# Attention outputs scaled by the softmax reciprocals once a group, instead of the probabilities head by head

## The reference

```
L0: self-attention "a0" (16 heads of 16, latent keys and values, scores times exp(-0.01 |i-j|))
    cross-attention on 64 context rows, butterfly feed-forward
L1: self-attention "a1" (16 heads of 64, rotary position, causal)
    attention "x1" (8 heads of 64, keys and values of x and of the 64 context rows)
    mixture of experts (8 experts, top 2)

attention:  p = softmax(scale * q k^T)      one row of probabilities per query
            out = (p v) W_o
```

## Time and profile before

| | us |
|---|---|
| median of 3 runs (4370.3 to 4377.9) | 4376.41 |
| the profiled execution's own time | 4397.46 |
| its span | 4395.7 |
| stage a0, about | 17 to 955 |
| cross-attention, folding, feed-forward, about | 955 to 1462 |
| stage a1, about | 1462 to 2590 |
| stage x1, about | 2590 to 3400 |
| experts and the rest | 3400 to 4396 |
| PE busy, mean granted clock | 3439.4 (78%), 0.898 |
| DVE, ACT, POOL busy | 2820.9, 2073.9, 1385.9 |

### The profile page before, as it was taken

The page is one execution under the profiler, slowest core; times in us unless marked ns, Lnnn a source line. Parts: engine busy times, 40 slices in busy tenths (PEclk is TensorE's granted clock), DMA queues, the critical chain, the costliest instruction groups (busy, mean ns, idle before and its releaser), DMA issues. The chain is left out here.

```text
span 4395.7 us, 81705 instructions
## 1 busy us (share of the span) xinstructions
PE 3439.4 (78%) x25420; PEld 2507.5 (57%) x25421; DVE 2820.9 (64%) x7262; ACT 2073.9 (47%) x4994; POOL 1385.9 (32%) x1108
## 2 busy tenths in 40 slices
PE   5878788758689588888888879999998409999970
PEld 3555555537678356666556556777767306666650
DVE  5888888868867488888888846666666311121116
ACT  4777777753242165555555536555555101111110
POOL 1333333324300376666665702122222350000004
PEclk9999999988799799999899989999999559999995
DMA  2000000010010211111111110000000720010013
GB/s 68 6 7 7 7 7 7 1 34 19 25 74 1 66 44 35 30 44 37 35 40 31 33 41 7 11 6 6 6 1 1 242 80 27 29 31 29 29 35 105
DMA packets 101919, 147.71 MB, mean 34 GB/s; under 512 B 19904, under 2 KB 71552, under 8 KB 100800
## 3 DMA queue, kind: packets, MB, share of 16 engines
q1 hardware_dynamic: 95424, 126.58, 9.5%
q0 software_dynamic: 6144, 16.79, 1.2%
HBM read 61.52 MB, written 31.46 MB: 21 GB/s over the span
## 5 line engine op out<-in xcount | busy, mean ns | idle before, releaser
L1012 DVE TENSOR_SCALAR a_t<-a_t,a_inv 128x512 f32<-128x512 f32 (+3 forms) x768 | 719.1, 979 | 9.0
L695 PE MATMUL a_T<-ident,a_t 128*128 128x128 f32 x3328 | 535.3, 300 | 163.8 <-DVE a_t L1012 89.8
L854 ACT ACTIVATE a_t<-a_t,a_neg 128x512 f32<-128x512 f32 (+3 forms) x1024 | 642.5, 634 | 7.7 <-DVE a_neg L1040 7.3
L845 ACT ACTIVATE a_pT<-a_T 128x512 f32<-128x512 f32 (+3 forms) x1024 | 484.7, 514 | 328.1 <-PE a_T L695 324.6
L695 PEld LDWEIGHTS a_T<-ident,a_t 128*128 128x128 f32 x3328 | 402.7, 151 | 379.8 <-issue 217.0
L884 POOL TENSOR_TENSOR a_t<-a_t,a_inv 128x512 f32<-128x512 f32 x256 | 284.4, 1133 | 653.5 <-DVE a_inv L1008 653.5
L1035 DVE CUSTOM_DVE_ANT_0 a_t<-a_A,a_decay 128x512 f32<-128x512 f32 x512 | 322.7, 685 | 91.0 <-PE a_A L655 89.3
L884 POOL TENSOR_TENSOR x_t<-x_t,x_inv 128x576 f32<-128x576 f32 x128 | 158.1, 1257 | 696.3 <-DVE x_inv L1008 696.3
L2096 DVE COPY experts_y<-experts_Y 128x256 f32<-128x256 f32 x72 | 30.6, 425 | 513.9 <-PE experts_Y L2034 513.9
L909 POOL TENSOR_TENSOR a_rsin<-a_rawswapped,a_sin 128x512 f32<-128x512 f32 x128 | 170.1, 1329 | 583.5 <-DMA a_rawswapped<-a_raw 558.7
L1035 DVE CUSTOM_DVE_ANT_0 a_t<-a_A,a_table 128x384 f32<-128x384 f32 (+3 forms) x512 | 224.1, 485 | 128.5 <-PE a_A L667 125.6
(11 more groups left out here) (273 smaller groups left out, 7243.1 us busy)
## 6 DMA issues: line engine op xcount, KB each, us to landing
a_rawswapped<-a_raw SPq DMA_DIRECT2D x512, 64.0 KB, 2.0
ex_w<-in_f_w_dram SPq DMA_DIRECT2D x16, 1024.0 KB, 13.6
moe_sent<-route_zeros SPq DMA_DIRECT2D x1, 9216.0 KB, 29.5
experts_xg<-moe_sent SPq DMA_DIRECT2D x72, 128.0 KB, 2.0
moe_results<-experts_y SPq DMA_DIRECT2D x72, 128.0 KB, 1.7
a_xin<-x_all SPq DMA_DIRECT2D x16, 512.0 KB, 4.1
x_xin<-x_all SPq DMA_DIRECT2D x16, 512.0 KB, 2.9
x_all<-in_x_dram SPq DMA_DIRECT2D x1, 4096.0 KB, 14.9
```

What stands on the lines that cost most here:

```text
L695: mm = pe.transpose(bank[:, kt, :], t_of(u, j, kt * P, (kt + 1) * P), sh.ident[:])
L845: nc.scalar.activation(to, of, ACT.Copy).then_inc(t_empty, 1)
L854: nc.scalar.activation(t_of(u_e % U, j, 0, n), t_of(u_e % U, j, 0, n), ACT.Exp, bias=neg[:, slot, j:j + 1], scale=SCALE, accum_out=total[: ...
L1012: nc.vector.tensor_scalar(t_of(u_n % U, j, 0, m), t_of(u_n % U, j, 0, m), inv[:, u_n % 4, j:j + 1], None, ALU.mult).then_inc(normed, 1)
```

## The change

1. Nobody multiplies the probabilities. PE transposes them as soon as exp is done (it waits for `exped` instead of `normed`).
2. DVE still takes the reciprocals; `inv` now keeps all units of a batch. After each unit SP writes the 128x4 reciprocals to a table in DRAM, transposed, so that a row holds one head's 512 queries (`spill`). Once per SPAN units (8 in a0, 4 in a1 and x1) SP reads the rows back, each repeated over the partitions that the head's outputs take in O, into `inv_rep` (`spread_rows`: 8 transfers in a0, 2 otherwise), and waits for them.
3. The copy of O to `oT` moves from ACT to DVE and becomes a product with `inv_rep`. It stands after DVE's items of the step and before the score maxima, and waits for PE's product and for the spread.
4. SP's program becomes one list of steps: input load, spread, spill, then in a1 the swaps. POOL's program for a0 and x1 is gone.
5. The folding loads its weights in two parts a side, of 3 and 4 stages, not 2, 2 and 3.

```diff
@@ attention
-    POOL_HEADS = () if a1 else (2, 3)
-    DVE_HEADS = 4 - len(POOL_HEADS)
+    SPAN = 8 if a0 else 4
+    COPIES = 8 if a0 else 2
...
-        inv = sb("inv", [P, 4, 4])
+        inv = sb("inv", [P, U, 4])
+        inv_rep = sb("invrep", [P, 1 if a0 else 2, S])
+        inv_rows = nc.dram_tensor(f"{kind}_inv_rows", (2, SPAN, S), F32).ap()
...
+            def spill(b, u):
+
+                g, qt = divmod(u % U, QT)
+                rows = inv_rows[g // 2 % 2, g % 2::2] if a0 else inv_rows[g % 2]
+                wait_apart(sp, (weights, 16 * len(loads)), (inverted, b * U + (u + 1)))
+                sp.dma_start(rows[:, qt * P:(qt + 1) * P].rearrange("j p -> p j"), inv[:, u % U, :], allow_slow_non_contiguous=True)\
+                  .then_inc(spilled[u % U // SPAN % 2], 16)
+
+            def spread_rows(b, k):
+
+                per = U // SPAN
+                p = k % per % 2
+                wait_apart(sp, (weights, 16 * len(loads)),
+                           (spilled[p], b * (per // 2 * SPAN * 16) + (k // 2 + 1) * SPAN * 16))
+                for c in range(COPIES):
+                    if a0:
+                        to, of = inv_rep[16 * c:16 * c + 16, 0, :], inv_rows[p, c:c + 1, :].to_broadcast([16, S])
+                    else:
+                        to = inv_rep[64 * c:64 * c + 64]
+                        of = inv_rows[p, c::2, :].unsqueeze(0).to_broadcast([64, 2, S])
+                    sp.dma_start(to, of).then_inc(spread, 16)
+                wait_apart(sp, (weights, 16 * len(loads)), (spread, b * (per * COPIES * 16) + (k + 1) * COPIES * 16))
+
+            def step(b, s, prev, own, nxt):
+                if s == 0 and nxt:
+                    sp.wait_ge(xt_done, b * DT + DT)
+                    sp.dma_start(xin[:], sh.x_all[:, bass.ds(b * QT + QT, QT), :]).then_inc(xin_in, 16)
...
+                u_n = s - LAG_N
+                if s < U and u_n % SPAN == 0 and (own if u_n > 0 else prev):
+                    spread_rows(b, u_n // SPAN - 1)
+                if s < U and (own if u_n >= 0 else prev):
+                    spill(b, u_n)
+                for _, work in tasks(s, prev, own, nxt):
+                    if a1 and work[0] == "item":
+                        swap_halves(b + (work in NEXT and s >= U - QT), 4 * work[1] + work[2])
@@ PE, transpose_head
-                by_dve, by_pool = min(j + 1, DVE_HEADS), min(j + 1, 4) - DVE_HEADS
-                waits = [(normed, ug * DVE_HEADS + by_dve)] + \
-                    ([(normed_pool, ug * len(POOL_HEADS) + by_pool)] if by_pool > 0 else []) + [(t_empty, job + 1)]
...
+                wait_apart(pe, (ready, N_READY), (exped, ug * 4 + min(j + 1, 4)), (t_empty, job + 1))
@@ ACT, step
-                        act.wait_ge(pv, b * U + (u_v + 1 + 2))
-                        for o in ([g // 2] if a0 else [0, 1]):
-                            nc.scalar.activation(oT[:, o if a0 else 2 * g + o, :], O[o][:],
-                                                 ACT.Copy).then_inc(o_empty, 1)
@@ POOL: the step that multiplies heads 2 and 3, and its loop, are removed
@@ DVE, step
-                        nc.vector.reciprocal(inv[:, u_n % 4, :], total[:, u_n % 4, :]).then_inc(inverted, 1)
-                        dve.wait_ge(inverted, b * U + (u_n + 1))
-                    if do_n and j < DVE_HEADS:
-                        m = NK if x1 else keys(u_n % U)
-                        nc.vector.tensor_scalar(t_of(u_n % U, j, 0, m), t_of(u_n % U, j, 0, m),
-                                                inv[:, u_n % 4, j:j + 1], None, ALU.mult).then_inc(normed, 1)
+                        nc.vector.reciprocal(inv[:, u_n % U, :], total[:, u_n % 4, :]).then_inc(inverted, 1)
...
+                if do_v and u_v % SPAN == SPAN - 1:
+                    g = u_v % U // QT
+                    wait_apart(dve, (ready, N_READY), (pv, b * U + (u_v + 1 + 2)),
+                               (spread, (b * (U // SPAN) + (u_v + 1) // SPAN) * COPIES * 16))
+                    for o in ([g // 2] if a0 else [0, 1]):
+                        nc.vector.tensor_tensor(oT[:, o if a0 else 2 * g + o, :], O[o][:], inv_rep[:, 0 if a0 else o, :],
+                                                ALU.mult).then_inc(o_empty, 1)
                 if own:
 
                     dve.wait_ge(t_full, (b * U + s + 1) * T_UNIT)
@@ fold_butterflies
-        GROUPS_OF = ((0, 2), (2, 4), (4, 7))
+        GROUPS_OF = ((0, 3), (3, 7))
```

More of the change, by code:

```diff
@@ L331, in attention @@
         idle = {"a0": ("ctx_in", "v_done", "rot_sum", "rot_done", "biased", "q_low", "low", "kp"),
-                "a1": ("folded", "ctx_in", "kl_done", "kp", "q_low", "biased", "normed_pool", "hi"),
+                "a1": ("folded", "ctx_in", "kl_done", "kp", "q_low", "biased", "hi"),
                 "x1": ("folded", "a_act", "rot_sum", "rot_done", "kl_done", "low", "kp")}[kind]
@@ L419, in attention @@
         exped = sem("exped")
-        normed = sem("normed")
-        normed_pool = sem("normed_pool")
+        spilled = [env.sem(f"spilled{i}") for i in range(2)]
+        spread = sem("spread")
         t_full = sem("t_full")
@@ L496, in swap_halves @@
                                  raw[32 * (k ^ 1):32 * (k ^ 1) + 32, n % 4, :]).then_inc(swapped[n % 2], 16)
[L498 to L515, removed]
-                      .then_inc(ctx_in, 16)
+            def spill(b, u):
[4 more added lines that the diff above has]
+                  .then_inc(spilled[u % U // SPAN % 2], 16)
@@ new lines, in step @@
+            def step(b, s, prev, own, nxt):
+                if s == 0 and nxt:
+                    sp.wait_ge(xt_done, b * DT + DT)
+                    sp.dma_start(xin[:], sh.x_all[:, bass.ds(b * QT + QT, QT), :]).then_inc(xin_in, 16)
+                if x1 and s == LAG_V and nxt:
+                    sp.wait_ge(v_done, b * N_V + N_V)
+                    sp.dma_start(ctxT[:], w["ctxT"][bass.ds(b + 1, 1)].rearrange("a (t p) n -> p (a t) n", p=P))\
+                      .then_inc(ctx_in, 16)
+                u_n = s - LAG_N
[6 more added lines that the diff above has]
+                        swap_halves(b + (work in NEXT and s >= U - QT), 4 * work[1] + work[2])
@@ L518, in _, with begin, body @@
+            def begin():
+                for work in START:
+                    if a1 and work[0] == "item":
+                        swap_halves(0, work[2])
+            def body(seg, turn, b, prev, own, nxt):
+                for s in range(U if own else LN_STEP):
+                    step(b, s, prev, own, nxt)
+            batches(sp, begin, body)
         @block.tensor
@@ L877, in _ @@
         def _(pool):
[L878 to L883, removed]
-                        nc.gpsimd.tensor_tensor(t_of(u_n % U, j, 0, NK), t_of(u_n % U, j, 0, NK),
-                                                inv[:, u_n % 4, j:j + 1].to_broadcast([P, NK]),
-                                                ALU.mult).then_inc(normed_pool, 1)
-            def begin():
-                pool.wait_ge(ready, N_READY)
-            def body(seg, turn, b, prev, own, nxt):
-                for s in range(U if own else LN_STEP):
-                    step(b, s, prev, own, nxt)
-            if not a1:
-                batches(pool, begin, body)
             if a1:
@@ L940, in _ @@
             dve.sem_inc(a_dve, A_BANKS)
+            dve.sem_inc(o_empty, 2)
             def low_parts(seg, turn, b, g, i):
@@ L1002, in step @@
                 do_n = s < U and (own if u_n >= 0 else prev)
+                u_v = s - LAG_V
+                do_v = s < U and (own if u_v >= 0 else prev)
                 slot, qt, n = s % 4, s % QT, keys(s)
@@ L1402, in fold_butterflies @@
         T = [env.ps(f"T{i}", [P, S]) for i in range(2)]
-        GROUPS_OF = ((0, 2), (2, 4), (4, 7))
-        staged = [[sem(f"staged_{side}{i}") for i in range(3)] for side in ("up", "down")]
+        GROUPS_OF = ((0, 3), (3, 7))
+        staged = [[sem(f"staged_{side}{i}") for i in range(2)] for side in ("up", "down")]
         loaded_up = sem("loaded_up")
```

4 lines of the change are left out of this document (removed).

## The result

Measured side by side on one chip, the changed kernel takes 4725.99 us (median of four, 4715.43 to 4754.48), the kernel before 4373.35 (4366.06 to 4377.9): a ratio of 1.082, 95% interval 1.077 to 1.087. The forecast was 4181 us, its range ended at 4310. The profiled execution took 4722.31 us, with a span of 4720.5.

What follows compares the result with a forecast made beforehand. It took x1 as bound by PE, a0 and a1 by engines holding one another up. Terms -100 - 86 - 16 + 5 + 2 = -195 us took 4376.4 to 4181 us; range 4060 to 4310.

Steps and rivals of the forecast that it cites:

- part 6: Reciprocals by DMA: a spill lands in 4.2 us (ends 2.0 and 10), hidden, so 0; some 5 us at stage ends.
- Parts 1 and 2: Normalisations go, DVE scales outputs while emptying PSUM: DVE falls to 56.1 us a batch in a0, 64.7 a1, 40.5 x1.
- Part 3: a0: without waits for DVE a batch takes 96 us, not 108.5: -100 us (-140 to -44).
- Part 4: a1: a batch takes 121 us, not 131.7, with more waiting for POOL's rotation: -86 us (-158 to -14).
- Part 5: x1: PE's waits for the O copy and context score bank shrink, 2 us a batch: -16 us (-24 to +8).
- Stage ends and folding: Uncovered spill and spread at the stages' ends, +5 us; folding's larger first load, +2 us (0 to +4).
- Rival C: Spills' 4-byte writes cost 280 ns a piece, holding the rings 9 us and limiting steps: about 4750 us; chance 0.08.
- All three signs named for a wrong forecast: Spill over 7 us; DVE waiting for the spread in a0; ACT and PE in a0 each under 85% busy.

Runs made afterwards that it cites:

- e2: Changed kernel without spreads, products using ones; all 320 spills kept, DVE waiting for them only a group later: 1.062 of the kernel before, 4662.57 us.
- g1: Changed kernel without spreads, products using ones; only one spill in four kept (80 of 320), awaited a group later: 0.988 of the kernel before, 4344.31 us.
- e1: Changed kernel without spills and spreads, outputs multiplied by a table of ones: 0.959 of the kernel before, 4210.92 us.
- f1: Complete changed kernel, but DVE transposes reciprocals before spilling, once a span, in four transfers of 128-byte pieces: 0.961 of the kernel before, 4205.09 us.
- e4: Changed kernel with spreads and waits, but each spill writes 128 pieces of 16 B, giving queries wrong numbers: 0.963 of the kernel before, 4229.19 us.

## Why the prediction was wrong

**The step that failed** is part 6: "I take 4.2 and keep 2.0 and 10 as ends ... Hidden, thus 0 here", and "nothing of weight shares them". Both ends were ends for how late a spill lands. None asked what it does to others, and that is the term: 0.103 of 4390, some 450 us, in e2, where it isn't awaited. The landing was missed as well: 11.6 to 13.3 us in a0 of g1, above the upper end of 10, though a packet took 29 ns on average and not 70. The time of a packet, from which the 4.2 was worked out, tells neither. The chain of spill and spread is the smaller miss: 1.082 against 1.062.

**Parts 1 and 2 were right**, read in e1: DVE is busy 339.74 / 6 = 56.6 us a batch in a0 (56 forecast), 399.50 / 6 = 66.6 in a1 (65), 250.68 / 6 = 41.8 in x1 (41); the product of O takes 687 ns (679).

```profile
33.50:626.10 592.60, 485.90 (x5328) 321.27 (x5328) 339.74 (x1142) 480.85 (x1153) 0.00 (x0) 0.95 0.02 7
1418.10:2155.70 737.60, 636.85 (x4775) 450.66 (x4776) 399.50 (x1230) 438.40 (x1293) 510.68 (x386) 0.93 0.16 40
2457.00:2969.60 512.60, 487.64 (x3932) 369.99 (x3932) 250.68 (x1025) 303.53 (x695) 0.00 (x0) 0.99 0.02 8
```

**Part 3** (a0, 96 us a batch): 98.8 in e1, a gain of 82 us over the stage where 100 was forecast. PE's waits for low parts fell from 68.8 to 18.2, to a quarter where a third was said. **Part 4** (a1, 121): 122.9, a gain of 68 for 86. PE's wait for POOL's rotation grew from 5.4 to 48.3 / 6 = 8.1 us a batch (9 said), and it is PE's longest. **Part 5** (x1, 88): 85.4; the gain of 4.4 a batch is 35 us for 16. The three errors cancel in part, which is luck: -82 - 68 - 35 = -185, where the forecast had -202 for the three. **Stage ends and folding** (+5, +2) lie within what a comparison can tell: f1, with spills and spreads, stands 0.002 above e1. The folding's first load lands in 8.6 us where it was 7.3 (the 8.3 of the earlier trace rows is the median of two).

**Rival C**, with a chance of 0.08, named the transfer, the sign, the stage and nearly the time (4750). It was right that a spill takes long: its point of decision, 0.21 us a piece, is never reached by the packets (29 ns), but it is by the landing, 11.6 to 13.3 us over 32 pieces, 0.36 to 0.42 each; had I measured only packets, I would have ruled it out. Its mechanism, a lower limit for a step, is not what happens: in e2 a step of a0 takes 1223 / 128 = 9.6 us, less than such a spill, and in g1, where only one step in four has a spill, each still costs. The chance was low because the average price of a packet in the earlier trace rows was counted as evidence on a kind of write of which that row holds none.

All three signs named for a wrong forecast came: a spill takes over 7 us (above), ACT and PE in a0 are under 85% busy (56% and 66%), and in the stretch of a0 DVE waits for spreads, though only 4.3 us in all; in that of a1 it is 56.7.

The Trainium skill, "DMA: Bandwidth & Descriptors", section "Specifications", says that writes under 512 bytes become read-modify-write. As a warning it pointed at the right place. As a rule it does not tell these runs apart: 4 bytes every 8, 64 or 512 bytes are all under 512 and cost nothing here; only their landing differs, as said.

## What to carry to other kernels

Ask of a new transfer not only when it lands but what it does to all else: a small test in which it is issued and not awaited tells the two apart. Don't write a column of many partitions to DRAM as 4-byte pieces that touch; turn them first (0.21 us of DVE for 128x32) and write runs of 128 bytes, or at least keep the pieces from touching. An average over packets says nothing of a kind of packet that it doesn't contain, and the end of the packets in a trace isn't yet the end of the writes: look at when they report that they are done.

## What the hardware showed that was not expected

- 512 writes of 4 bytes that touch in DRAM, their packets recorded within 2.2 us of the issue, report their end only 11.6 to 13.3 us after it (a0 of g1). After 13 of 32 such spills PE, ACT and DVE stood together for over 2 us, in the case shown until 12.4 us after the issue, even inside one engine's own chain. Issued by GpSimd, in 16 packets of 128 bytes, they cost as much (a0 1221 us against 1223).
- 128 touching pieces of 16 bytes land in 1.4 us (e4), 512 pieces of 4 bytes in 1.8 when they lie 512 bytes apart and in 3.8 when it is 8.
- The same writes 8 bytes apart cost nothing that can be measured (0.960 and 0.962 against 0.959 with none), and no fewer packets are made.
- The cost isn't linear: 128 touching pieces 0.005, 256 0.014, 512 0.103 of the time; 512 with the heads 512 bytes apart in place of 2 or 4 KB 0.027; 512 in four transfers 0.133.
